# Where the bias of a mixture-of-experts block is put into its accumulators: ahead of all matmuls of a quarter, or token tile by token tile between them

## The chip, the cores and the metric

The kernel runs on the 8 cores of one Trainium2 chip. Each core works on two of the sixteen sequences, alone, with no exchange between cores. The metric is the device time in microseconds (us) of the slowest core.

## The reference, cut to what matters

```python
def ffn(x, Wg, We, be):                 # x: tokens x 1024; We: 8 experts x 1024 x 1024
    gate_logits = xt @ Wg.T
    vals, sel = top_k(gate_logits, 2)
    w = softmax(vals, axis=1)
    y = einsum('td,eod->teo', xt, We) + be[None]
    y_sel = take_along_axis(y, sel[:, :, None], axis=1)
    return einsum('tk,tko->to', w, y_sel)

xn = layernorm(x)
s = attention(xn, qw, kw, vw, ow)       # 16 heads, rotary, causal, 2048 tokens
g = silu(ffn(xn, Wg, We, be))
out = x + s * g
```

The kernel computes all eight experts for each token and weighs them with a matrix `wm` that is zero for the six that were not chosen. So the output of the block is `sum over e of wm[t,e] * (xn @ We[e].T)` plus the bias part `wm @ be`, and it is the bias part that this case is about.

## The kernel before

A core has 4096 tokens, 32 tiles of 128. The program is one list of instructions, written out in order; `W(engine, instruction, waits, inc)` appends to it (line 57, `emit`), and each engine then runs its own in that order. A wait is on a count of a semaphore: `eT` counts TensorE's instructions, `eA` ScalarE's, `eV` VectorE's, and each transfer family has one of its own. A wait for a count that the same engine has already waited for is dropped.

Three stages follow one another with barriers between them:

1. Layer norm, transposition of the tokens into `xnT`, the projections to q, k and v, the rotary embedding, and then the gate's logits and weights `wm` (lines 243 to 614).
2. The experts (lines 625 to 706), which are the stage of the change.
3. Attention, the output projection and the product with the gate (from line 713).

In stage 2 a loop over `q4` takes four quarters of 8 token tiles. The accumulators `acc32[t8]` (128 tokens x 1024 f32, eight of them) live in SBUF. A quarter has three parts:

- **Bias phase**, lines 629 to 642: for each of the 8 tiles and 2 halves (512 columns) TensorE multiplies an 8-row weight matrix `wmT` with the 8x512 bias `be16s` into the one PSUM tile `PC6` (L632), and ScalarE copies `PC6` into the accumulator (L637). Since there is one `PC6`, each of the 16 matmuls waits for the copy before it (`("eA", C["eA"])`), and each copy for its matmul. `bias_done` is the count of the 16th copy.
- **Expert passes**, lines 643 to 696: `eg` takes two experts at a time. SyncE's queue brings their weights with 16 transposing transfers (L654, in the profile as SPq L237) into a pair of slots; there are two pairs, so pass `eg` uses the pair that pass `eg-2` left. The first matmul of a pass waits for all 16 (`(swx, wrd)`). Each of the 8 tiles and 2 halves then takes 16 matmuls of 128x128 by 512 columns (L677), in turn into `PA` and `PB`, and VectorE adds the two results with their gate weights to the accumulator (L687). In the first pass (`eg == 0`) the first matmul of a half also waits for `bias_done`, and so does VectorE.
- **Gate phase**, lines 697 to 706: ScalarE takes the SiLU of each accumulator (L701) into one of two staging tiles, and SyncE's queue stores it to `g_sp` (in the profile as SPq L238). A SiLU waits until the store of two tiles ago has landed.

ScalarE's order is: 8 SiLUs of a quarter, then the 16 copies of the next one. SyncE's order is: 8 stores of a quarter, then the transfers of the first pass of the next one, which have their slots free since pass 2 of the quarter before.

Of the kernel before, what the change touches and what calls it, by code (L numbers as in the profile page):

```python
# [107 lines left out]
def build_nc():  # L108
# [24 lines left out]
    with ctx:  # L133
# [33 lines left out]
        acc32 = [c32(AR2, 65536 + 4096 * i, 1024) for i in range(8)]  # L167
# [17 lines left out]
        wmT = sbt("wmT", [8, NT * 128], F16)  # L185
# [4 lines left out]
        be16s = sbt("be16s", [8, D], F16)  # L190
# [27 lines left out]
        PC6 = ctx.enter_context(nc.psum_tensor("PC6", [128, 512], F32))[:]  # L218
# [12 lines left out]
        W = P.emit  # L231
        C = P.cnt

        def dma(q, out, in_, sem, transpose=False, waits=()):
# [6 lines left out]
        tok = {}  # L241
# [14 lines left out]
          waits=[("scst", cst)], inc="eV")  # L256
        W("vector", lambda e: e.tensor_sub(wgr[0:8, :], wgf[0:8, :],
                                           wgs[0:8, 0:D]),
          waits=[("eV", C["eV"])], inc="eV")
        W("vector", lambda e: e.tensor_copy(wgs[0:8, D:2 * D], wgr[0:8, :]),  # L260
          waits=[("eV", C["eV"])], inc="eV")
        W("vector", lambda e: e.tensor_sub(wgr[0:8, :], wgr[0:8, :],
                                           wgs[0:8, D:2 * D]),
          waits=[("eV", C["eV"])], inc="eV")
        W("vector", lambda e: e.tensor_copy(wgs[0:8, 2 * D:3 * D], wgr[0:8, :]),
          waits=[("eV", C["eV"])], inc="eV")
        wg_split = C["eV"]
        for c in range(NCH):
            for s3 in range(3):
# [5 lines left out]
                  waits=[("eV", wg_split), ("scst", cst), ("eA", C["eA"])],  # L275
                  inc="eT")
# [4 lines left out]
                  waits=[("eT", C["eT"])], inc="eA")  # L281
# [261 lines left out]
        for t in range(NT):  # L543
            for c in range(NCH):
                for s3 in range(3):
# [5 lines left out]
                          start=(c == 0 and s3 == 0),  # L551
                          stop=(c == NCH - 1 and s3 == 2)),
                      waits=[("eA", max(C["eA"] if t == 0 and c == 0 and s3 == 0 else 0, wgT_done))], inc="eT")
        W("vector", lambda e: e.tensor_copy(lgall[:, :], PC6[:, 0:256]),
          waits=[("eT", C["eT"]), ("eV", C["eV"])], inc="eV")
# [3 lines left out]
          waits=[("eT", C["eT"]), ("eV", C["eV"])], inc="eV")  # L559
        W("vector", lambda e: e.reduce_max(v1a[:, :], d3(lgall), axis=AX.X),  # L560
          waits=[("eV", C["eV"])], inc="eV")
        W("vector", lambda e: e.tensor_tensor(
            d3(eq16[:, 0:256]), d3(lgall), bc(v1a[:, :]), op=ALU.is_equal),
          waits=[("eV", C["eV"])], inc="eV")
# [60 lines left out]
        bew = C["sbe"]  # L625
        wew = C["swe"]
        slot_free = {}
        for q4 in range(4):
            for t8 in range(8):
                gt = q4 * 8 + t8  # L630
                for half in range(2):
                    W("tensor", lambda e, gt=gt, half=half: e.matmul(  # L632
                        PC6[:, :], wmT[0:8, gt * 128:(gt + 1) * 128],
                        be16s[0:8, half * 512:(half + 1) * 512],
                        start=True, stop=True),
                      waits=[("sbe", bew), ("eA", C["eA"])], inc="eT")
                    W("scalar", lambda e, t8=t8, half=half: e.copy(  # L637
                        acc32[t8][:, half * 512:(half + 1) * 512],
                        PC6[:, :]),
                      waits=[("eT", C["eT"]),  # L640
                             ("eA", tok.get(("accfree", t8), 0))], inc="eA")
            bias_done = C["eA"]
            for eg in range(4):
                e0, e1 = 2 * eg, 2 * eg + 1
                sp = eg % 2
                slots = (weT[2 * sp], weT[2 * sp + 1])
                swx = "sweA" if sp == 0 else "sweB"
                ldw = [("eT", max(slot_free.get(sp, 0), loopT)),
                       ("eV", loopV), ("eP", loopP), ("swe", wew),
                       ("scsA", C["scsA"]), ("scsB", C["scsB"]),  # L650
                       ("scsC", C["scsC"]), ("scsD", C["scsD"])]
                for (sl, ee) in ((slots[0], e0), (slots[1], e1)):
                    for c in range(NCH):
                        dma("sync", sl[:, c * D:(c + 1) * D],  # L654
                            we16[ee, :, c * 128:(c + 1) * 128], swx,
                            transpose=True, waits=ldw)
                        ldw = []
                wrd = C[swx]
                for t8 in range(8):
                    gt = q4 * 8 + t8  # L660
                    for half in range(2):
                        bk = (t8 * 2 + half) % 2
                        PG = PA if bk == 0 else PB
                        for c in range(NCH):
                            lhs = xnT[:, c * T + gt * 128:
                                      c * T + (gt + 1) * 128]
                            for ib in range(2):
                                wts = [(swx, wrd)]
                                if c == 0:
                                    wts.append(  # L670
                                        ("eV", tok.get(("pbfree", 2 * bk + ib),
                                                       0)))
                                    if eg == 0 and ib == 0:
                                        wts.append(("eA", bias_done))
                                W("tensor",
                                  lambda e, ib=ib, lhs=lhs, c=c, PG=PG,
                                  sl=slots[ib], half=half: e.matmul(  # L677
                                      PG[:, 512 * ib:512 * ib + 512], lhs,
                                      sl[:, c * D + half * 512:
                                         c * D + (half + 1) * 512],  # L680
                                      start=(c == 0), stop=(c == NCH - 1)),
                                  waits=wts, inc="eT")
                        mm = C["eT"]
                        for ib, ee in ((0, e0), (1, e1)):
                            W("vector",
                              lambda e, ib=ib, t8=t8, half=half, PG=PG,
                              gt=gt, ee=ee: e.scalar_tensor_tensor(  # L687
                                  acc32[t8][:, half * 512:(half + 1) * 512],
                                  PG[:, 512 * ib:512 * ib + 512],
                                  wm32[:, gt * 8 + ee:gt * 8 + ee + 1],  # L690
                                  acc32[t8][:, half * 512:(half + 1) * 512],
                                  op0=ALU.mult, op1=ALU.add),
                              waits=[("eT", mm), ("eA", bias_done),
                                     ("eV", C["eV"])], inc="eV")
                            tok[("pbfree", 2 * bk + ib)] = C["eV"]
                slot_free[sp] = C["eT"]
            for t8 in range(8):
                gt = q4 * 8 + t8
                p = gt % 2
                sg_ = "sgsA" if p == 0 else "sgsB"  # L700
                W("scalar", lambda e, t8=t8, p=p: e.activation(  # L701
                    g_st[p][:, :], acc32[t8][:, :], AF.Silu),
                  waits=[("eV", C["eV"]), (sg_, 16 * (gt // 2))], inc="eA")
                tok[("accfree", t8)] = C["eA"]
                dma("sync", g_sp[gt * 128:(gt + 1) * 128, :], g_st[p][:, :],
                    sg_, waits=[("eA", C["eA"])])
# [294 lines left out]
```

How the kernel before makes its waits and increments, by code:

```python
            def body(eng):  # L84
                for (e, ws, fn, incs) in ops:
                    if e != name:
                        continue
                    for (sn, v) in ws:
                        eng.wait_ge(sems[sn], v)
                    if fn is None:
                        if incs:
                            ins = eng.drain()
                            for (sn, a) in incs:
                                ins.then_inc(sems[sn], a)
                        continue
                    ins = fn(eng)
                    for (sn, a) in incs:
                        ins.then_inc(sems[sn], a)
```

## Time and profile before

| | |
|---|---|
| time, median of 3 runs | 2890.38 us (2868.5, 2890.38, 3182.27) |
| profiled execution, its own time | 2858.58 us |
| its span, slowest core (core 3) | 2857.0 us |
| spans of the eight cores | 2838.1 to 2857.0 us |
| TensorE matmul busy | 2176.7 us (76%) |
| VectorE, ScalarE, GpSimd busy | 35%, 34%, 16% |
| stage 2 (experts), from the first bias matmul to the end of the last matmul | 587 to 1634 us |

The span runs from the first to the last instruction of the slowest core. In the rows PE is TensorE's matmuls, PEld its weight loads, DVE is VectorE, ACT ScalarE, POOL GpSimd, and SPq the queue in which SyncE issues transfers. The granted clock of TensorE is given as a share of full speed: 1.00 is 2.4 GHz, 0.50 is 1.2 GHz. "Idle before <- X" is the time for which the engine stood still before this instruction, and what ended it.

### The profile page before, as it was taken

To read this page: it belongs to the slowest core of one execution; us is meant where nothing else is said; L and a number is where in the kernel's file an instruction comes from. 1 tells how busy PE (TensorE), PEld (TensorE's weight loads), DVE (VectorE), ACT (ScalarE), POOL (GpSimd) and SP (SyncE) were. 2 spreads that over 40 slices of the span, in tenths; PEclk is the share of its full clock that TensorE was granted. 3 is DMA by queue.
4 is the path that set the end of the run, shared out by engine and by line. 5 is a ranking of instruction groups with operands and counts; after the bars stand their busy time and mean duration, and the time that the engine had idled before them with its cause. 6 is when DMAs were issued, how large, how long until landed. Compare 5 with 4: busy or idle time off the path is not lost.

```text
span 2857.0 us, 30318 instructions; the slowest of 8 cores (2838.1 to 2857.0 us)
## 1 busy us (share of the span) xinstructions
PE 2176.7 (76%) x9976; PEld 818.2 (29%) x9976; DVE 996.4 (35%) x1529; ACT 961.7 (34%) x1373; POOL 461.2 (16%) x543
## 2 busy tenths in 40 slices
PE   1888788569977995999599806777788347677787
PEld 0333333424433442444144301121211102121211
DVE  3675776424422442344144303231201213221212
ACT  2444443110010002000200015657587134657574
POOL 0465665300000000000000002211111021211110
PEclk9999999679988997999699955888898757788888
DMA  4299842714416524560743080211010532020100
GB/s 130 75 164 169 156 107 85 125 29 60 60 44 104 78 41 89 80 97 1 132 75 59 14 218 6 74 42 32 14 46 1 136 72 74 1 74 1 59 1 30
DMA packets 382533, 203.94 MB, mean 71 GB/s; under 512 B 342944, under 2 KB 351136, under 8 KB 381872
## 3 DMA queue, kind: packets, MB, share of 16 engines
q1 hardware_dynamic: 370160, 142.76, 25.5%
q0 software_dynamic: 12224, 59.27, 9.7%
q8 instruction: 85, 1.39, 0.2%
q14 instruction: 64, 0.52, 0.1%
HBM read 84.28 MB, written 67.37 MB: 53 GB/s over the span
## 4 chain that ended last, share of the span: by engine, by line
PE 60%; ACT 12%; issue 7%; SPq 7%; POOL 5%; DVE 4%; DMA 3%; ACTq 0%; POOLq 0%; DVEq 0%
PE PA L677 16%; PE PB L677 15%; ACT AR L861 9%; SPq L237 6%; PE PV L780 6%; POOL AR L872 5%; PE PA L906 5%; PE PA L419 4%; PE PB L419 4%; PE PC L419 4%; PE PA L851 2%; PE PB L851 2%; ACT AR L790 2%; PE PV L359 1%; DMA AR<-c_sin 1%
## 5 line engine op out<-in xcount | busy, mean ns | idle before, releaser
L677 PE MATMUL PA<-AR 128*128 128x512 f16 x2048 | 472.1, 384 | 22.4 <-DMA AR<-we 21.5
L780 PE MATMUL PV<-AR 128*128 128x512 f16 (+6 forms) x1280 | 417.0, 417 | 66.7 <-POOL AR L872 66.6
L677 PE MATMUL PB<-AR 128*128 128x512 f16 x2048 | 462.9, 379 | 0.0
L861 ACT ACTIVATE AR<-PA 128x1024 f16<-128x1024 f32 x320 | 303.1, 947 | 249.3 <-PE PA L851 247.1
L851 PE MATMUL PA<-AR 64*128 64x512 f16 x640 | 148.6, 455 | 292.1 <-ACT AR L861 142.4
L687 DVE SCALAR_TENSOR_TENSOR AR<-PA,wm,AR 128x512 f32<-128x512 f32 x256 | 192.2, 751 | 416.4 <-PE PA L677 226.2
L861 ACT ACTIVATE AR<-PB 128x1024 f16<-128x1024 f32 (+1 forms) x320 | 276.2, 863 | 90.3 <-PE PB L851 89.6
L872 POOL TENSOR_TENSOR AR<-AR,tri 128x256 f16<-128x256 f16 x256 | 170.7, 667 | 814.9 <-ACT AR L861 791.0
L677 PEld LDWEIGHTS PA<-AR 128*128 128x128 f16 x2048 | 202.5, 99 | 271.8 <-issue 36.4
L687 DVE SCALAR_TENSOR_TENSOR AR<-PB,wm,AR 128x512 f32<-128x512 f32 x256 | 192.2, 751 | 250.3 <-PE PB L677 232.2
L822 DVE TENSOR_TENSOR AR<-AR,PC 64x512 f16<-64x512 f32 x64 | 43.5, 680 | 662.4 <-PE PC L816 661.3
L701 ACT ACTIVATE AR<-AR 128x1024 f16<-128x1024 f32 x32 | 32.1, 1049 | 711.3 <-DVE AR L687 696.1
L677 PEld LDWEIGHTS PB<-AR 128*128 128x128 f16 x2048 | 200.4, 98 | 241.6
L419 PE MATMUL PC<-AR 128*128 128x512 f16 x512 | 194.8, 380 | 0.0
L238 POOL DMA_DIRECT2D AR<-v_sp x2 | 2.4, 1196 | 1143.9 <-ACTq L92 1118.9
L851 PEld LDWEIGHTS PA<-AR 64*128 64x128 f16 x640 | 36.3, 96 | 465.0 <-issue 464.2
L419 PE MATMUL PA<-AR 128*128 128x512 f16 x512 | 160.3, 394 | 0.0
L802 DVE COPY AR<-PV 64x1024 f32<-64x1024 f32 x64 | 77.9, 1217 | 233.0 <-PE PV L780 227.2
L780 PEld LDWEIGHTS PV<-AR 128*128 128x128 f16 (+1 forms) x1280 | 83.3, 104 | 264.3 <-issue 264.0
L419 PE MATMUL PB<-AR 128*128 128x512 f16 x512 | 156.2, 385 | 0.0
L906 PE MATMUL PA<-AR 128*128 128x512 f16 x512 | 133.9, 421 | 17.5 <-DVE AR L828 14.8
L851 PE MATMUL PB<-AR 64*128 64x512 f16 x640 | 146.9, 453 | 0.0
(99 smaller groups left out, 1693.2 us busy)
## 6 DMA issues: line engine op xcount, KB each, us to landing
we<-we POOLq DMA_DIRECT2D x8, 2048.0 KB, 23.8
out_c<-AR SPq DMA_DIRECT2D x8, 2048.0 KB, 9.1
v_sp<-AR POOLq DMA_DIRECT2D x32, 264.0 KB, 3.5
AR<-v_sp POOLq DMA_DIRECT2D x2, 4224.0 KB, 26.3
AR<-x_c SPq DMA_DIRECT2D x32, 256.0 KB, 11.6
k_sp<-AR POOLq DMA_DIRECT2D x32, 256.0 KB, 4.4
q_sp<-AR SPq DMA_DIRECT2D x32, 256.0 KB, 3.7
g_sp<-AR SPq DMA_DIRECT2D x32, 256.0 KB, 2.0
```

The lines of the kernel that those rows point to most:

```text
L237: return e.dma_start(out, in_, transpose=True)
L419: e.matmul(o_, lhs, rhs, start=(c == 0), stop=(c == NCH - 1)),
L677: sl=slots[ib], half=half: e.matmul(PG[:, 512 * ib:512 * ib + 512], lhs, sl[:, c * D + half * 512: c * D + (half + 1) * 512], start=(c == ...
L687: gt=gt, ee=ee: e.scalar_tensor_tensor(acc32[t8][:, half * 512:(half + 1) * 512], PG[:, 512 * ib:512 * ib + 512], wm32[:, gt * 8 + ee:gt * ...
L780: nkc=nkc, p2=p2, mw=mw: e.matmul(PV2[0:mw, 512 * p2 + w0:512 * p2 + 512], v_sb[:, kc * VF + h * VW:kc * VF + h * VW + mw], expb3[sbk][:, ...
L790: W("scalar", lambda e: e.activation(recL[64:65, 0:1024], PV2[64:65, 0:1024], AF.Ln), waits=[("eT", pvmm), ("eA", C["eA"]), ("eA", tok.get ...
L802: W("vector", lambda e: e.tensor_copy(at2[0:64, :], PV2[0:64, 0:1024]), waits=[("eT", pvmm), ("eV", tok.get("atrd", 0))], inc="eV")
L822: W("vector", lambda e, hp=hp: e.tensor_mul(attnT[0:64, hp * 512:(hp + 1) * 512], at2[0:64, 0:512], PC6[0:64, :]), waits=[("eV", tok[("atv ...
L851: pbuf=pbuf, PS=PS, p2=p2: e.matmul(PS[:, 512 * p2:512 * p2 + 512], kT[base:base + 64, ch * S + kc * 128:ch * S + (kc + 1) * 128], qT[pbuf ...
L861: W("scalar", lambda e, PS=PS, sbk=sbk, ev=ev: e.activation(ev(expb3[sbk]), ev(PS), AF.Exp, scale=1.0 / 32.0), waits=[("eT", C["eT"]), ("e ...
L872: W("gpsimd", lambda e, sbk=sbk, tv=tv: e.tensor_mul(tv(expb3[sbk]), tv(expb3[sbk]), tri[:, :].unsqueeze(1).broadcast_to([128, 2, 128])), ...
L906: e.matmul(PA[:, 512 * half:512 * half + 512], attnT[0:128, cp * 512 + jt * 128: cp * 512 + (jt + 1) * 128], ow128[:, cp * D + half * 512: ...
```

## The change

The bias matmul and its copy move into a small function `bias_init(t8, half)`, which is called twice for each tile inside the first expert pass, just ahead of that tile's matmuls. The bias phase at the head of a quarter is gone. The single wait for `bias_done` becomes a wait for the copy of the tile and half in question. Numbers and kinds of instructions stay: 64 bias matmuls and 64 copies over the program; `PC6` stays the one PSUM tile for both halves, so the second bias matmul of a tile waits for the copy of the first.

```diff
         for q4 in range(4):
-            for t8 in range(8):
+            def bias_init(t8, half, q4=q4):
                 gt = q4 * 8 + t8
-                for half in range(2):
-                    W("tensor", lambda e, gt=gt, half=half: e.matmul(
-                        PC6[:, :], wmT[0:8, gt * 128:(gt + 1) * 128],
-                        be16s[0:8, half * 512:(half + 1) * 512],
-                        start=True, stop=True),
-                      waits=[("sbe", bew), ("eA", C["eA"])], inc="eT")
-                    W("scalar", lambda e, t8=t8, half=half: e.copy(
-                        acc32[t8][:, half * 512:(half + 1) * 512],
-                        PC6[:, :]),
-                      waits=[("eT", C["eT"]),
-                             ("eA", tok.get(("accfree", t8), 0))], inc="eA")
-            bias_done = C["eA"]
+                W("tensor", lambda e, gt=gt, half=half: e.matmul(
+                    PC6[:, :], wmT[0:8, gt * 128:(gt + 1) * 128],
+                    be16s[0:8, half * 512:(half + 1) * 512],
+                    start=True, stop=True),
+                  waits=[("sbe", bew), ("eA", C["eA"])], inc="eT")
+                W("scalar", lambda e, t8=t8, half=half: e.copy(
+                    acc32[t8][:, half * 512:(half + 1) * 512],
+                    PC6[:, :]),
+                  waits=[("eT", C["eT"]),
+                         ("eA", tok.get(("accfree", t8), 0))], inc="eA")
+                tok[("accinit", t8, half)] = C["eA"]
...
                 for t8 in range(8):
                     gt = q4 * 8 + t8
+                    if eg == 0:
+                        bias_init(t8, 0)
+                        bias_init(t8, 1)
                     for half in range(2):
...
                                     if eg == 0 and ib == 0:
-                                        wts.append(("eA", bias_done))
+                                        wts.append(
+                                            ("eA", tok[("accinit",
+                                                        t8, half)]))
...
-                              waits=[("eT", mm), ("eA", bias_done),
+                              waits=[("eT", mm),
+                                     ("eA", tok[("accinit", t8, half)]),
                                      ("eV", C["eV"])], inc="eV")
```

## Rows read from the trace of the kernel before

**Rows 1.** The page, parts 1, 2 and 4: busy time, slices, chain by engine.
```profile
PE 2176.7 (76%) x9976; PEld 818.2 (29%) x9976; DVE 996.4 (35%) x1529; ACT 961.7 (34%) x1373; POOL 461.2 (16%) x543
...
PE   1888788569977995999599806777788347677787
...
PE 60%; ACT 12%; issue 7%; SPq 7%; POOL 5%; DVE 4%; DMA 3%; ACTq 0%; POOLq 0%; DVEq 0%
```

**Rows 2.** Groups by line in stage 2: busy and mean; idle before, releasers.
```profile
L677 PE MATMUL PA<-AR 128*128 128x512 f16 x2048 | 472.1, 384 | 22.4 <-DMA AR<-we 21.5 <-ACT AR L637 0.8
L637 ACT COPY AR<-PC 128x512 f32<-128x512 f32 x64 | 37.5, 586 | 54.7 <-PE PC L632 54.7
L632 PE MATMUL PC<-be16s,wmT 8*128 8x512 f16 x64 | 37.1, 580 | 95.3 <-ACT AR L637 50.9 <-ACT AR L701 43.0 <-POOLq L92 1.4
```

**Rows 3.** Timeline of the first bias phase and first matmuls: start, us, engine, line.
```profile
587.05 0.58 PE L632 MATMUL PC<-be16s,wmT 8*128 8x512 f16 x1 [1.41 <-POOLq L92]
587.72 0.59 ACT L637 COPY AR<-PC 128x512 f32<-128x512 f32 x1 [1.73 <-PE PC L632]
...
588.45 0.58 PE L632 MATMUL PC<-be16s,wmT 8*128 8x512 f16 x1 [0.82 <-ACT AR L637]
...
609.45 5.53 PE L677 MATMUL PA<-AR 128*128 128x512 f16 x16 [0.82 <-ACT AR L637]
...
618.27 3.62 PE L677 MATMUL PA<-AR 128*128 128x512 f16 x16
618.61 1.60 DVE L687 SCALAR_TENSOR_TENSOR AR<-PB,wm,AR 128x512 f32<-128x512 f32 x2 [1.78 <-PE PB L677]
```

**Rows 4.** Timeline between the first and the second quarter, all engines.
```profile
836.82 11.15 SPq L238 DMA_DIRECT2D g_sp<-AR  x8
...
845.58 2.01 ACT L701 ACTIVATE AR<-AR 128x1024 f16<-128x1024 f32 x2 [1.29 <-DMA g_sp<-AR]
847.70 0.10 PEld L632 LDWEIGHTS PC<-be16s,wmT 8*128 8x128 f16 x1 [15.66 <-issue]
847.73 0.58 PE L632 MATMUL PC<-be16s,wmT 8*128 8x512 f16 x1 [15.19 <-ACT AR L701]
...
869.88 0.59 ACT L637 COPY AR<-PC 128x512 f32<-128x512 f32 x1 [0.82 <-PE PC L632]
...
878.12 6.02 PE L677 MATMUL PA<-AR 128*128 128x512 f16 x16 [8.33 <-DMA AR<-we]
```

**Rows 5.** Chain that ended last, 864 to 880 us: start, us, what.
```profile
871.07 1.87 SPq L237
...
872.99 4.78 DMA AR<-we
877.77 0.35 issue
878.12 2.29 PE PA L677 x5
```

**Rows 6.** Who waited for whom, second and third of these boundaries: us, times, longest.
```profile
PE PC L632 <- ACT AR L637: 13.0, 15, 1.2
...
PE PA L677 <- DMA AR<-we: 5.9, 1, 5.9
...
PE PC L632 <- ACT AR L637: 12.8, 15, 0.9
...
PE PA L677 <- DMA AR<-we: 7.3, 1, 7.3
```

**Rows 7.** Line 677 by line: durations min/median/max and first and last start.
```profile
L677 PE MATMUL PA<-AR x2048: 379/379/634, 609.4 to 1630.5; 128*128 128x512 f16 x187
```

**Rows 8.** Chain that ended last, whole span: one half's matmuls at full clock.
```profile
618.43 3.45 PE PA L677 x16
```

**Rows 9.** Windows: span, PE, PEld, DVE, ACT, POOL busy, granted clock, DMA share, GB/s.
```profile
300.00:400.00 100.00, 87.30 (x412) 38.64 (x411) 75.11 (x122) 45.84 (x101) 63.08 (x62) 1.00 0.80 151
...
586.00:609.00 23.00, 9.25 (x16) 1.60 (x16) 0.00 (x0) 9.07 (x16) 0.00 (x0) 0.50 0.00 0
...
870.00:878.00 8.00, 0.00 (x0) 0.00 (x0) 0.00 (x0) 0.46 (x1) 0.00 (x0) 0.50 1.22 161
878.10:883.00 4.90, 4.88 (x12) 1.87 (x13) 0.00 (x0) 0.00 (x0) 0.00 (x0) 0.50 1.10 180
883.00:933.00 50.00, 50.00 (x233) 22.63 (x232) 21.36 (x29) 0.00 (x0) 0.00 (x0) 1.00 0.33 61
...
1999.40:2002.50 3.10, 2.98 (x8) 0.50 (x8) 0.00 (x0) 2.58 (x3) 0.00 (x0) 0.50 0.00 0
```

**Rows 10.** Timeline of TensorE in stage 1, between two tiles of projections.
```profile
307.32 0.27 PE L359 MATMUL PV<-idn,AR 128*128 128x128 f16 x2
308.01 0.35 PE L359 MATMUL PV<-idn,AR 128*128 128x128 f16 x2 [0.42 <-DVE AR L370]
309.45 0.39 PE L359 MATMUL PV<-idn,AR 128*128 128x128 f16 x2 [1.09 <-ACT AR L369]
310.15 0.39 PE L359 MATMUL PV<-idn,AR 128*128 128x128 f16 x2 [0.31 <-DVE AR L370]
```

**Rows 11.** Timeline of TensorE in stage 3, around the tail of a head pair.
```profile
1996.13 0.37 PE L816 MATMUL PC<-AR,ones 1*64 1x512 f16 x1
1996.43 0.39 PE L851 MATMUL PA<-AR 64*128 64x512 f16 x2
1996.66 0.38 PE L851 MATMUL PB<-AR 64*128 64x512 f16 x2
1999.52 0.61 PE L851 MATMUL PA<-AR 64*128 64x512 f16 x2 [2.48 <-ACT AR L861]
```

**Rows 12.** Timeline of SyncE's queue, several stretches: start, us, transposing transfers.
```profile
848.07 24.87 SPq L237 DMA_TRANSPOSE AR<-we  x15
...
666.87 24.36 SPq L237 DMA_TRANSPOSE AR<-we  x15
...
936.01 22.62 SPq L237 DMA_TRANSPOSE AR<-we  x16
...
529.15 52.75 SPq L237 DMA_TRANSPOSE AR<-we  x32
```

## The prediction

> **What bounds the kernel now.** I read the page first: its busy times, its slices and the shares of the chain [rows 1]. TensorE is busy for 76% of the span and carries 60% of the chain, and the slices show it at 9 through the middle of the run, which is the expert stage, with single dips. No other engine passes 35%. So in the expert stage I ask only where TensorE stands still.
>
> The groups by line answer that [rows 2]. Over the stage the big matmuls L677 wait 22.4 us in all, and 21.5 of them for the expert weights. The bias matmuls L632 wait 50.9 us for the copy before them and 43.0 us for the SiLUs. The reader is to see that the copies' 50.9 us look like the prize, and that a second releaser, the weights, ends the wait of L677 after them.
>
> So the timelines come next, at two kinds of place. **First quarter** [rows 3]: the first bias matmul starts at 587.05, the next at 588.45, a cycle of 1.40 us, and the sixteenth copy lets the first big matmul go at 609.45. That is 16 x 1.40 = 22.4 us in which TensorE waits for nothing but this chain: SyncE's queue had issued the first 32 weight transfers from 529.15 to 581.90 [rows 12], and in the bias phase the DMA share is 0.00 [rows 9]. **The three later quarters**, of which the second stands for all [rows 4]: the last SiLU lets the first bias matmul go at 847.73, the last copy ends at 870.47, and still the first big matmul starts only at 878.12, 8.33 us after TensorE could have, released by the weights. The chain of waits shows the same from the other end [rows 5]: back from 878.12 it goes to the landing of a weight transfer, to SyncE's queue, and never touches the bias phase. In the other two boundaries the weights come 5.9 and 7.3 us after the bias [rows 6]. The sum of the three, 21.5 us, is the 21.5 of [rows 2]. The queue can't start earlier: the transfers stand behind the eight stores of the gate, the last of which is issued when the last SiLU is done [rows 4].
>
> **The change part by part.**
>
> *Removed: the bias phase in front of each quarter.* In quarter one it takes 22.4 us off the path. In quarters two to four it takes nothing off: the bias ran in the shade of the weights, from 847.73 to 870.47, and without it the first big matmul still waits for 878.12. That cover is what makes the old place cheap there.
>
> *Added: a pair of bias matmuls and copies in front of each tile of the first pass.* TensorE is in order, so behind the second bias matmul of a tile stand the 32 big matmuls of that tile, and behind them VectorE. The steps for one tile, at full clock:
> - the first bias matmul follows the matmuls before it directly; its wait was met a tile ago. A 512-column matmul takes 0.38 us from start to end then [rows 7]; the bias matmul itself shows 0.58, but only at half clock [rows 3, 9].
> - 0.09 us to the copy (588.45 minus 0.14 minus 0.59 is 587.72, and the matmul ends at 587.63), the copy 0.59, and 0.14 to the second bias matmul [rows 3].
> - So start to start 0.38 + 0.09 + 0.59 + 0.14 = 1.20 us.
> - the second bias matmul holds the stream for one slot: 3.45 / 16 = 0.216 us [rows 8]. Its copy runs under the first half's 16 big matmuls (3.45 us against about 0.7) and the second half finds it done.
>
> Together 1.41 us a tile. The first tile of a quarter is apart: in quarters two to four its pair runs before the weights land and costs nothing. In quarter one it runs at half clock: 1.40 + 0.43 = 1.83 us.
>
> *Moved waits.* VectorE and the big matmuls get one wait more per half, already met. VectorE stands still for 1.78 us of each 3.45 [rows 3], so it never comes late. ScalarE has nothing else to do in a pass. No transfer is issued in another order; the weights of the third pass start when the first pass ends, some 10 us later on the clock but at the same distance from their use.
>
> *The sum.*
> - Quarter one: -22.4 + 1.83 + 7 x 1.41 = -10.7 us.
> - Quarters two to four: 3 x 7 x 1.41 = +29.6 us.
> - Together +18.9 us, or 28 x c + 1.8 - 22.4 with c = 1.41.
>
> *Bounds of the unshown cost c.* No row shows a bias matmul inside a running stream. From below it is 1.41: each term is the shortest of its kind in the trace. A gain is excluded, since the wait of the second matmul for the copy is in the code. From above I take the half-clock pair, 1.83, and two changes between a small and a full weight tile at 0.09 each (the matmul at 1996.43 stands 0.30 behind a one-row matmul at 1996.13 where a slot is 0.216 [rows 11]): 2.0 us. That gives 28 x 2.0 + 1.8 - 22.4 = +35.4 us. I take 1.41, since the row it is nearest to is the full-clock stream.
>
> *The clock.* TensorE's clock falls to half after long idle: it is at 0.50 through 870 to 878 and for the first 4.9 us of matmuls after it [rows 9]. The new stalls are 0.82 us long (1.20 less the matmul's 0.38), one in about 8.3 us. In stage 1 TensorE has idle stretches of 0.42, 1.09 and 0.31 us between two tiles [rows 10], and the clock is 1.00 over 300 to 400 [rows 9], with 87% busy. In stage 3 a wait of 2.48 us [rows 11] is followed by 3.1 us at 0.50 [rows 9]. The new stall is shorter than the 1.09 us that stage 1 shows at 1.00. I cost it at nothing and keep the fall as a rival.
>
> The Trainium skill, "TensorE: Matmul & The Clock Gate", section "A second HAM failure mode: psum-queue depth-cycling", speaks against this change: it says that a TensorE which often idles briefly between groups of matmuls, because of how PSUM is cycled, can swing between half and full clock and lose throughput. By that rule the sum would be that of the rival "the clock falls" below; stage 1, with its brief idle stretches at 1.00, doesn't bear it out.
>
> **Which total.** The profiled execution took 2858.6 us, its span and 1.6 us around it. The three runs gave 2868.5, 2890.4 and 3182.3; I leave the last out as disturbed. The mean of the other two and the profiled one is 2872.5, which is 14 above the profiled time and 18 below the median. I add to that: 2872.5 + 18.9 = **2891.4 us**. Against the profiled time alone it would be 2877.5, against the median 2909.3; the spread of the base is wider than the effect.
>
> **The rivals.**
> - *All four bias phases come off the path.* This is what the 50.9 us of [rows 2] suggest: -4 x 22.4 + 4 x 1.83 + 28 x 1.41 = -42.8, so 2829.7 us, 1.5% faster. It decides where weights land before the bias is done. Against it: the weights were last at three of three boundaries, by 8.3, 5.9 and 7.3 us. This is the case on the other side. Chance 3%.
> - *The weights land sooner once bias and copies are out of their way.* Beside the bias phase 15 transfers were issued in 24.87 us, 1.66 each; at 936.01 sixteen took 22.62, 1.41 each [rows 12]. At best 15 x 0.25 = 3.7 us a boundary, 11 in all: +8 instead of +19, 2880 us. Against it: at 666.87, beside full matmuls and no bias, 15 took 24.36. To turn the sign it would need 6.3 us a boundary. Chance 12%.
> - *The clock falls in the stalls.* A return from half clock costs 9 to 12 matmuls at 0.21 us more each (5.53 us for sixteen at 609.45 [rows 3] against 3.45 is 2.1; 6.02 at 878.12 [rows 4] is 2.6). At 28 stalls that is 59 to 73 us on top of 18.9, 78 to 92: about 2957 us, 3.0% slower. Against it: stage 1. For it: the 2.48 us case. It decides where the granted clock of the first passes shows below 1.00. Chance 7%.
>
> **How the numbers follow.** My forecast, +18.9 to +35.4, has 78%. The predicted time is 2891 us. For the range: low is the smallest base with the weights-sooner case, 2858.6 + 8 = 2866; high is the largest undisturbed base with the upper bound of c, 2890.4 + 35.4 = 2926. Outside are the 3%, the 7%, and some 8% for executions that drift further (the clock in stage 3 wanders, and a shift of its start may move it). 2% of 2890 is 58 us, about what a measurement of this kernel can tell from no change. Neither my forecast nor the first two rivals reach it; only the clock does. So faster 2%, within 2% 90%, slower 8%.
>
> **What would show it.** In the profile of the changed kernel:
> - the first big matmul of quarter one starts near 589, not 609;
> - at the three later boundaries it is still released by the weights, and the wait named there grows from 21.5 us to about 21.5 + 3 x 21 = 85 us, since TensorE now stops 14 matmuls earlier;
> - inside each first pass TensorE waits some 0.8 us for L637, once a tile, and the first pass takes about 10 us more than the second;
> - the granted clock stays at 1.00 in it.
> It would be wrong if the stall of a tile is much over 1.4 us, if the clock in the first pass is below 1.00, or if the first big matmul of the later quarters comes closer to the last SiLU than 30 us.

## The result, and the profile after

The changed kernel is slower by 1%: its time is 1.0097 times that of the kernel before, 95% interval 1.0069 to 1.0126. On a base of 2872 us, the one used in the prediction, that is +28 us (20 to 36). The medians of 42 executions each are 2909.32 us after and 2888.37 us before; some executions of either kernel are held up by a lower clock on one die, and the ratio leaves these out.

| | before | after |
|---|---|---|
| profiled execution, its own time | 2858.58 us | 2880.76 us |
| its span, slowest core | 2857.0 us (core 3) | 2879.2 us (core 0) |
| stage 1, to the first bias matmul, mean of eight cores | 583.3 us | 579.0 us |
| stage 2, from there to the start of the last half's big matmuls | 1040.2 us | 1066.6 us |
| stage 3, the rest | 1225.0 us | 1226.7 us |
| big matmuls waiting for weights, mean of eight cores | 16.3 us | 76.3 us |

The three stages are read from the first and last starts of the bias and of the big matmuls on each core, so stage 3 here begins with the last quarter's gate phase. The whole loss is in stage 2: +26.4 us.

First the groups by line in stage 2 of the changed kernel (busy, mean ns, idle before and its releasers). L681 is the big matmul, L631 the bias matmul, L636 its copy; they answer to [rows 2].

```profile
L681 PE MATMUL PA<-AR 128*128 128x512 f16 x2048 | 473.0, 385 | 77.6 <-DMA AR<-we 77.6
...
L636 ACT COPY AR<-PC 128x512 f32<-128x512 f32 x64 | 37.5, 585 | 302.5 <-PE PC L631 302.5
```

Line 631 by itself, on the same core: durations and what its engine waited for.

```profile
L631 PE MATMUL PC<-be16s,wmT x64: 371/384/581, 588.6 to 1484.8; 8*128 8x512 f16 x64
...
  ACT AR L706: 42.5, 3
  ACT AR L636: 27.9, 32
```

Two things moved against [rows 2]. The wait for the copies fell from 50.9 us to 27.9, as the change meant. The wait for the weights rose from 21.5 (core 3) to 77.6 (core 0): TensorE only reaches it earlier.

The timeline shows where the time went. First quarter, core 0, all engines (start, us, engine, line), to be laid beside [rows 3]:

```profile
588.64 0.58 PE L631 MATMUL PC<-be16s,wmT 8*128 8x512 f16 x1 [1.44 <-POOLq L92]
...
590.56 5.68 PE L681 MATMUL PA<-AR 128*128 128x512 f16 x16
...
599.62 0.38 PE L631 MATMUL PC<-be16s,wmT 8*128 8x512 f16 x1
...
600.10 0.58 ACT L636 COPY AR<-PC 128x512 f32<-128x512 f32 x1 [8.80 <-PE PC L631]
600.80 0.09 PEld L631 LDWEIGHTS PC<-be16s,wmT 8*128 8x128 f16 x1 [1.09 <-issue]
600.83 0.37 PE L631 MATMUL PC<-be16s,wmT 8*128 8x512 f16 x1 [0.82 <-ACT AR L636]
601.13 3.14 PEld L681 LDWEIGHTS PA<-AR 128*128 128x128 f16 x16 [0.24 <-issue]
601.13 3.63 PE L681 MATMUL PA<-AR 128*128 128x512 f16 x16
...
604.38 3.33 PEld L681 LDWEIGHTS PB<-AR 128*128 128x128 f16 x16
604.60 3.62 PE L681 MATMUL PB<-AR 128*128 128x512 f16 x16
...
609.65 3.14 PEld L681 LDWEIGHTS PA<-AR 128*128 128x128 f16 x16 [0.24 <-issue]
609.66 3.63 PE L681 MATMUL PA<-AR 128*128 128x512 f16 x16
```

The first big matmul comes 1.92 us after the first bias matmul, where it was 22.4. From then on a tile takes 8.52 us (601.13 to 609.65) and two halves of big matmuls fill 6.91 of them, so the pair costs c = 1.61 us.

Second quarter, TensorE on core 3, to be laid beside [rows 4]:

```profile
830.36 0.58 PE L631 MATMUL PC<-be16s,wmT 8*128 8x512 f16 x1 [15.05 <-ACT AR L706]
831.82 0.58 PE L631 MATMUL PC<-be16s,wmT 8*128 8x512 f16 x1 [0.88 <-ACT AR L636]
856.66 6.02 PE L681 MATMUL PA<-AR 128*128 128x512 f16 x16 [24.26 <-DMA AR<-we]
862.52 3.62 PE L681 MATMUL PB<-AR 128*128 128x512 f16 x16
866.07 0.39 PE L631 MATMUL PC<-be16s,wmT 8*128 8x512 f16 x1
867.33 0.37 PE L631 MATMUL PC<-be16s,wmT 8*128 8x512 f16 x1 [0.88 <-ACT AR L636]
867.63 3.63 PE L681 MATMUL PA<-AR 128*128 128x512 f16 x16
```

The bias phase is gone and the weights are last all the same, 26.3 us after the first bias matmul. The other seven pairs now stand behind them, each with a stop of 0.88 us. That it was 0.82 in the first quarter is a matter of the quarter and not of the core; core 0 in the second quarter:

```profile
880.01 0.37 PE L631 MATMUL PC<-be16s,wmT 8*128 8x512 f16 x1 [0.88 <-ACT AR L636]
880.32 3.63 PE L681 MATMUL PA<-AR 128*128 128x512 f16 x16
```

All eight cores have c = 1.61 us in the first quarter and 1.67 in the later ones. Why the step from copy to matmul is 0.06 us longer there was not looked into. The clock in this pass and in the next one, as windows (span, busy times, granted clock after the last "x0)"):

```profile
866.00:925.00 59.00, 52.86 (x235) 22.29 (x235) 21.02 (x28) 8.21 (x14) 0.00 (x0) 1.00 0.23 41
925.00:978.00 53.00, 53.00 (x247) 24.01 (x246) 22.51 (x30) 0.00 (x0) 0.00 (x0) 1.00 0.48 80
```

It stays at 1.00 through the stops.

### The profile page after: what moved, and what is told of

Its sections match the earlier page's. It is cut to its first block, busy times and chain, and to the rows that moved or that the text cites. A ratio compares the mean times of both kernels' runs of the same rounds, so it can differ in the third digit from the quotient of the medians.

```text
span 2879.2 us, 30378 instructions; the slowest of 8 cores (2867.2 to 2879.2 us)
## 1 busy us (share of the span) xinstructions
PE 2166.5 (75%) x9976; PEld 814.9 (28%) x9976; DVE 990.7 (34%) x1529; ACT 962.3 (33%) x1373; POOL 462.1 (16%) x543
## 4 chain that ended last, share of the span: by engine, by line
PE 60%; ACT 13%; issue 7%; SPq 7%; POOL 5%; DVE 4%; DMA 3%; ACTq 0%; POOLq 0%; DVEq 0%
PE PA L681 16%; PE PB L681 15%; ACT AR L866 8%; PE PV L785 6%; SPq L237 6%; POOL AR L877 5%; PE PA L911 5%; PE PA L419 4%; PE PB L419 4%; PE PC L419 4%; PE PA L856 2%; PE PB L856 2%; ACT AR L795 2%; PE PV L359 1%; DMA AR<-c_sin 1%
## 5 line engine op out<-in xcount | busy, mean ns | idle before, releaser
L681 PE MATMUL PA<-AR 128*128 128x512 f16 x2048 | 473.0, 385 | 77.6 <-DMA AR<-we 77.6
L681 PE MATMUL PB<-AR 128*128 128x512 f16 x2048 | 462.9, 379 | 0.0
L681 PEld LDWEIGHTS PA<-AR 128*128 128x128 f16 x2048 | 200.3, 99 | 327.6 <-issue 99.1
L681 PEld LDWEIGHTS PB<-AR 128*128 128x128 f16 x2048 | 200.4, 98 | 241.6
L911 PE MATMUL PA<-AR 128*128 128x512 f16 x512 | 133.6, 420 | 16.3 <-DVE AR L833 14.4
## 6 DMA issues: line engine op xcount, KB each, us to landing
we<-we POOLq DMA_DIRECT2D x8, 2048.0 KB, 25.7
```

Of the source, the lines that this page charges most:

```text
L681: sl=slots[ib], half=half: e.matmul(PG[:, 512 * ib:512 * ib + 512], lhs, sl[:, c * D + half * 512: c * D + (half + 1) * 512], start=(c == ...
L911: e.matmul(PA[:, 512 * half:512 * half + 512], attnT[0:128, cp * 512 + jt * 128: cp * 512 + (jt + 1) * 128], ow128[:, cp * D + half * 512: ...
```

## The experiments

The kernels are variants of the changed one unless it is said otherwise. Lengths of stages are means over the eight cores of the profiled execution, as in the table above. A summary first:

| | ratio to before, 95% interval | stage 2 | against before's 1040.2 |
|---|---|---|---|
| changed kernel | 1.0097 [1.0069, 1.0126] | 1066.6 us | +26.4 |
| e1, change in quarter one only | 0.9963 [0.9924, 1.0003] | 1032.2 us | -8.0 |
| e2, change in quarters two to four only | 1.0104 [1.0033, 1.0175] | 1073.3 us | +33.1 |
| e3, one bias matmul per half, no stop for the copy | 1.0009 [0.9970, 1.0048] | 1046.3 us | +6.1 |
| e5, kernel before with early weights | 0.9945 [0.9888, 1.0003] | 1026.8 us | -13.4 |
| e6, changed kernel with early weights | 0.9866 [0.9768, 0.9965] | 989.7 us | -50.5 |
| e7, e3 with early weights and early SiLU | 0.9618 [0.9549, 0.9688] | 929.4 us | -110.8 |
| e9, e7 without the wait for the SiLU | 0.9465 [0.9341, 0.9588] | 913.4 us | -126.8 |

### e1 and e2: the change cut in two

The condition is `q4 > 0` in e1, as shown, and `q4 == 0` in e2: where it holds, the bias phase stays in front.

```diff
+            if q4 > 0:
+                for t8 in range(8):
+                    bias_init(t8, 0)
+                    bias_init(t8, 1)
...
-                    if eg == 0:
+                    if eg == 0 and not (q4 > 0):
```

> The change in the first quarter alone; quarters two to four keep the bias phase in front. Theory (the weights hide the phase in the later quarters, each tile of the stream costs c): the first quarter's 22.4 us give way to 1.9 us for the cold first pair and 7 x 1.61 us read from the changed kernel, so 9 us faster than before, ratio 0.997. The wait of the big matmuls for the weights stays what it was, about 15 to 21 us in three. Rival (the +28 us come from elsewhere than the later quarters, as from attention or from ScalarE): no faster than before, ratio 1.00 to 1.01.

> The change in quarters two to four alone; the first quarter keeps its bias phase in front. Theory: 3 x 7 tiles x 1.65 us = 35 us slower than before, less up to 2 us if the weights land a little sooner, ratio 1.012; together with e1 it makes the whole change (35 - 9 = 26). Rival (weights land much sooner without the bias beside them): under 25 us slower, and the first big matmul comes under 25 us after the first bias matmul.

Measured: e1's stage 2 is 8.0 us shorter than before, e2's 33.1 us longer. They add to +25.1, the changed kernel's own +26.4 within what cores differ by. So the change is a gain of some 8 us in the one quarter whose bias phase nothing hid, and a loss of 33 us, 11 a quarter, in the three where the weights hid it. The groups by line show the weights' wait, in e1 as in [rows 2], in e2 as in the changed kernel; the first row is e1's, the second e2's:

```profile
L688 PE MATMUL PA<-AR 128*128 128x512 f16 x2048 | 471.9, 384 | 21.3 <-DMA AR<-we 21.3
```

```profile
L688 PE MATMUL PA<-AR 128*128 128x512 f16 x2048 | 472.4, 384 | 79.1 <-DMA AR<-we 78.3 <-ACT AR L636 0.8
```

The ratio of e1 alone can't be told from 1; it is its stage 2 that carries the verdict. e2's can. In e2 the loss is under the 35 us expected but over the rival's 25. What is missing is the weights: they let the first big matmul go 26.7 us after the first bias matmul, in the mean of cores and boundaries, against 27.6 before, which makes 2.6 us over three boundaries.

### e3: what in a pair costs time

```diff
-                    if eg == 0:
-                        bias_init(t8, 0)
-                        bias_init(t8, 1)
                     for half in range(2):
+                        if eg == 0:
+                            bias_init(t8, half)
...
-                                    if eg == 0 and ib == 0:
-                                        wts.append(
-                                            ("eA", tok[("accinit",
-                                                        t8, half)]))
```

> As the changed kernel, but one bias matmul stands before each half (not two before a tile) and the big matmuls no longer wait for the copy, which only VectorE needs. Nothing is left out. Theory (the stall for the copy of the one PSUM tile is 0.82 us of the 1.61, and two changes of weight tile size at about 0.18 a bias matmul the rest): a tile costs 2 x 0.40 = 0.79 us, no wait for ScalarE in the passes; first quarter -16 us, later ones +18 us, so within 3 us of before and 25 us faster than the changed kernel, ratio to before 1.000 to 1.001. Rival (the cost is the matmuls' place and not their wait): it stays 24 us or more slower than before.

Measured: ratio 1.0009, stage 2 +6.1 us against before, 20.3 us shorter than in the changed kernel. TensorE in the first quarter:

```profile
603.02 3.63 PE L676 MATMUL PA<-AR 128*128 128x512 f16 x16
606.58 0.39 PE L631 MATMUL PC<-be16s,wmT 8*128 8x512 f16 x1
606.90 3.63 PE L676 MATMUL PB<-AR 128*128 128x512 f16 x16
610.46 0.39 PE L631 MATMUL PC<-be16s,wmT 8*128 8x512 f16 x1
610.78 3.63 PE L676 MATMUL PA<-AR 128*128 128x512 f16 x16
```

No row has a wait. A half takes 3.88 us (603.02 to 606.90) instead of 3.45, so a bias matmul costs 0.43 us and a tile 0.85, where 0.79 was expected. So spreading the pair and dropping the stop saves 1.61 to 1.67 less 0.85, 0.76 to 0.82 us a tile. What remains, 0.43 us for a matmul whose slot is 0.216, is twice the slot, and that is the question of the next experiment. Stage 2 was expected within 3 us of before and is 6 above: 32 x 0.06 = 1.9 us of that is the dearer bias matmul, and 1.8 the weights, which were last 0.6 us later a boundary than before (28.2 against 27.6).

### e4 and e8: 8 rows against 128

```diff
-                    PC6[:, :], wmT[0:8, gt * 128:(gt + 1) * 128],
-                    be16s[0:8, half * 512:(half + 1) * 512],
+                    PC6[:, :], xnT[:, gt * 128:(gt + 1) * 128],
+                    xnT[:, half * 512:(half + 1) * 512],
```

> As the changed kernel, but the matmul of the bias uses 128 rows of the tokens instead of the 8 rows of the gate weights and the bias, so the accumulators start from a wrong value; same place, same waits, same 512 columns. Theory (about 0.09 us is lost at each change between an 8-row and a 128-row weight tile, since the weight load isn't pulled ahead): spacing of the second of the pair to the next big matmul falls from 0.30 to 0.22 us, a tile from 1.61 to about 1.44 us. Rival (the 0.18 us belong to the wait or to the change of PSUM tile): spacing stays 0.30.

The records of e4 are from an execution at a granted clock of 0.81 in the expert passes, so its spacings can't be laid beside the changed kernel's. The same kernel was taken once more:

> The same kernel as e4 (accumulators start from a wrong value), taken once more, since e4's records are at a granted clock of 0.81. At 1.00 in the first pass, theory (change between weight tiles of 8 and of 128 rows costs): the second of the pair is followed by the next big matmul after 0.22 us or less (0.30 in the changed kernel), the first follows the stream at once, a tile costs about 1.44 us. Rival: 0.30 and 1.61 to 1.67 us as in the changed kernel.

e8, core 3, TensorE in the second quarter, at 1.00, to be laid beside the changed kernel's rows of the same core above:

```profile
868.13 0.38 PE L631 MATMUL PC<-AR 128*128 128x512 f16 x1 [0.88 <-ACT AR L636]
868.35 3.61 PE L681 MATMUL PA<-AR 128*128 128x512 f16 x16
871.80 3.62 PE L681 MATMUL PB<-AR 128*128 128x512 f16 x16
875.25 0.38 PE L631 MATMUL PC<-AR 128*128 128x512 f16 x1
876.51 0.38 PE L631 MATMUL PC<-AR 128*128 128x512 f16 x1 [0.88 <-ACT AR L636]
876.73 3.61 PE L681 MATMUL PA<-AR 128*128 128x512 f16 x16
```

The second of the pair is followed after 0.22 us (0.30 in the changed kernel), the first starts one slot behind the stream (871.80 + 3.45 = 875.25; in the changed kernel 862.52 + 3.45 = 865.97 and the start at 866.07), and a tile takes 8.38 us, c = 1.47, against 8.56 to 8.58 and 1.67 in this quarter. The stop of 0.88 us is the same. So 0.20 us of c are the two changes between a weight tile of 8 rows and one of 128. In the changed kernel's rows of the first quarter it can be seen how: the weight load of the big matmul behind the pair starts at 601.13, together with its matmul, where in the running stream it goes ahead (604.38 for the matmul at 604.60). In e8 it goes ahead behind the pair too, 0.12 us before the matmul at 868.35:

```profile
868.23 3.24 PEld L681 LDWEIGHTS PA<-AR 128*128 128x128 f16 x16
```

With that every part of c is measured: two slots (0.43), two changes of weight tile (0.20), and the stop. The stop costs more than the 0.76 to 0.82 that e3 saved, because e3's two separate bias matmuls pay four changes of weight tile where the pair pays two. The second matmul of the pair starts 1.20 us (first quarter) or 1.26 us (later) after the first, instead of 0.216, so the stop takes 0.98 or 1.05 us. Stage 2 of e8 is 1061.3 us, 5.3 less than the changed kernel's, where 28 x 0.20 = 5.6.

### e5 and e6: is the place bad, or the weights?

In both, the transfers for a quarter's first pass are issued before the stores of the gate, at the head of pass four, as soon as pass three has left their slots.

```diff
+                if not (q4 > 0 and eg == 0):
+                    load_w(eg)
                 wrd = C[swx]
+                if eg == 3 and q4 < 3:
+                    load_w(0)
```

> As the kernel before, with one thing moved: the weight transfers of a quarter's first pass are issued ahead of the eight stores of the gate, at the end of pass three, so that they land under pass four. Theory (weights were last at the three later boundaries by 5 to 8 us and the bias is next behind them): the wait of the big matmuls for weights goes to 0, they are released by the last copy, and the gain is only 15 to 21 us, ratio 0.993. Rival (the transfers cost the same elsewhere, by slowing the stores or pass four): no gain.

> As the changed kernel, with the same move of the weight transfers. Theory (the weights are all that made the old place of the bias free): now the removed bias phase is time on the path, each later boundary loses about 26 us and keeps 7 x 1.65 us in the pass; against before 3 x (-28 + 2) + 35 - 9 = -52 us, ratio 0.982; against e5, the same change is worth about -36 us where it cost 28. Rival (the change is bad in itself): e6 slower than e5.

e5, groups by line: the wait for weights is gone and the last copy releases the big matmuls, four times:

```profile
L698 PE MATMUL PA<-AR 128*128 128x512 f16 x2048 | 470.9, 384 | 3.3 <-ACT AR L652 3.3
```

Stage 2 is 13.4 us shorter. That is before's 16.3 us of waiting for weights less 3 x 0.8 for the copies that are last now: the bias phase had ended some 5 us ahead of the weights, so no more was to be had from them.

e6, TensorE between the first and the second quarter:

```profile
809.22 3.62 PE L691 MATMUL PB<-AR 128*128 128x512 f16 x16
828.07 0.58 PE L647 MATMUL PC<-be16s,wmT 8*128 8x512 f16 x1 [15.24 <-ACT AR L716]
829.53 0.58 PE L647 MATMUL PC<-be16s,wmT 8*128 8x512 f16 x1 [0.88 <-ACT AR L652]
830.04 5.82 PE L691 MATMUL PA<-AR 128*128 128x512 f16 x16
```

The first big matmul now comes 1.97 us after the first bias matmul, close to the 1.92 of quarter one. Stage 2 is 50.5 us shorter than before (52 expected). The same change, laid on the kernel with early weights, gives 1026.8 - 989.7 = 37 us; laid on the kernel as it was, it took 26. This is the case's main finding, and it is shown: neither the pairs nor their stops differ between the two (from first to last big matmul the four quarters grow by 46.5 us over e5's here, and by 47.2 over before's in the changed kernel), only what stood behind the bias phase. The ratio of e6 (0.9866, 38 us) is less than its stage 2 says: stage 3 took 1233.5 us in the profiled executions of e5 and e6, 8.5 more than before, with the same instructions (more on that at the end).

### e7 and e9: all of it together

The SiLU and the store of a tile stand right behind its last addition in pass four; the loop over them at the end of a quarter is gone.

```diff
+                    if eg == 3:
+                        p = gt % 2
+                        sg_ = "sgsA" if p == 0 else "sgsB"
+                        W("scalar", lambda e, t8=t8, p=p: e.activation(
+                            g_st[p][:, :], acc32[t8][:, :], AF.Silu),
+                          waits=[("eV", C["eV"]), (sg_, 16 * (gt // 2))],
+                          inc="eA")
+                        tok[("accfree", t8)] = C["eA"]
+                        dma("sync", g_sp[gt * 128:(gt + 1) * 128, :],
+                            g_st[p][:, :], sg_, waits=[("eA", C["eA"])])
```

> The spread bias of e3, the early weights of e5, and the SiLU and store of a tile right behind its last addition in pass four. Nothing is left out. Theory: TensorE no longer stops between quarters (42 to 46 us each, and about 2.4 us of half clock after each), nor for the last eight SiLUs (11 us), nor for the first bias phase (22 us), and pays 32 x 0.79 = 25 us: about 145 us faster than before, ratio 0.95. Rival (something else is next, stores and weights of eight cores at once or VectorE): under 100 us.

Measured: ratio 0.9618, about 109 us (89 to 129), stage 2 -110.8 us, and the mean span of the cores 122 us under before's. In the 122 is what the last eight SiLUs gave, which lie outside stage 2: the last one ends 3.3 us after the last big matmul, where it was 13.7. That is short of the 145 expected, and over the rival's 100 by stage 2 and the spans, though the interval of the ratio reaches below it. The boundary shows the main cause:

```profile
819.47 3.62 PE L686 MATMUL PB<-AR 128*128 128x512 f16 x16
826.21 0.37 PE L647 MATMUL PC<-be16s,wmT 8*128 8x512 f16 x1 [3.13 <-ACT AR L709]
826.52 5.31 PE L686 MATMUL PA<-AR 128*128 128x512 f16 x16
```

TensorE still stops for 3.13 us (3.1 to 3.4 at the three boundaries), for the SiLU of the last tile, and its clock falls: sixteen matmuls take 5.31 us and not 3.45. Three times both is about 15 us of the 23 that are missing. A smaller part is that the three boundaries of the kernel before, from the last big matmul of a quarter to the first of the next, come to 125 us, and the expectation counted 42 to 46 each. The stop shown above, as windows:

```profile
816.00:823.00 7.00, 7.00 (x33) 3.04 (x31) 3.00 (x4) 1.06 (x1) 0.00 (x0) 1.00 0.11 39
826.20:829.00 2.80, 2.79 (x7) 0.96 (x8) 0.00 (x0) 0.59 (x1) 0.00 (x0) 0.57 0.64 155
829.00:831.80 2.80, 2.80 (x12) 1.08 (x10) 0.00 (x0) 0.00 (x0) 0.00 (x0) 0.82 1.07 102
```

That stop is no need of TensorE's: the bias matmul waits for all that ScalarE had been given, and needs only its PSUM tile. In e9 `tok["pc6"]` is the count of the last copy out of `PC6`.

```diff
-                  waits=[("sbe", bew), ("eA", C["eA"])], inc="eT")
+                  waits=[("sbe", bew), ("eA", tok["pc6"])], inc="eT")
```

> As e7, but a bias matmul waits only for the last copy out of its own PSUM tile and not for all that ScalarE was given before it, the SiLU above all. Nothing is left out. Theory (after e7 the 3.1 us that TensorE stands still for the SiLU at each boundary are the last stop between quarters, and only VectorE needs that order): the wait for the SiLU goes, TensorE stops under 1.5 us a boundary, 6 to 9 us faster than e7, ratio to before 0.958 to 0.960. Rival (PSUM: the first sums of a quarter wait for VectorE instead): same time as e7, with the wait moved to the big matmuls.

```profile
803.84 3.62 PE L688 MATMUL PB<-AR 128*128 128x512 f16 x16
807.39 0.39 PE L648 MATMUL PC<-be16s,wmT 8*128 8x512 f16 x1
807.71 3.63 PE L688 MATMUL PA<-AR 128*128 128x512 f16 x16
811.27 0.39 PE L648 MATMUL PC<-be16s,wmT 8*128 8x512 f16 x1
```

The boundary has vanished: 0.10 us beyond the slot. Stage 2 is 16.0 us shorter than e7's, twice what was expected, since the expectation had the stops (3 x 3.1) and left out the clock (3 x 1.9). Both together are 15. With a ratio of 0.9465, 5% under the kernel before, e9 is the best version here; by the mean spans of the profiled executions, 2718.7 against 2848.6 us, it is 4.6%.

## Why the prediction was right, point by point

The forecast of +18.9 us, with +35.4 as its upper bound, met +28 by the ratio and +26.4 in stage 2; the mechanism was right and one term was too small.

- *The bias phase was on the path in quarter one alone.* Right, by e1 and by the timelines. The first pair cost 1.92 us where 1.83 was said.
- *The weights stay last at the three later boundaries.* Right: their wait rose by 60.0 us in the mean of the cores (16.3 to 76.3), where 63 was said. The total said, 85 us, was too high only because it started from core 3, the core that had waited longest (21.5 us against a mean of 16.3). One reading was a little off: the big matmul could not have started 8.33 us earlier, since its copy ended 0.8 us into that wait. The cover was 7.5 us there and (16.3 - 3 x 0.8) / 3 = 4.6 us in the mean, which is what e5 got back.
- *c = 1.41 us a tile.* Too small; it measured 1.61 in the first quarter and 1.67 in the later ones. This is the term that was mis-sized. The prediction held the two changes of weight tile of 0.09 us in its upper bound and not in its value; e8 shows them to be real, 0.20 us together. The rest, in the later quarters, is the step from copy to matmul, 0.88 us there and 0.82 in the first. With these the sum becomes 7 x 1.61 + 21 x 1.67 + 1.9 - 22.4 = +25.8, and stage 2 measured +26.4.
- *The clock holds.* Right: 1.00 through a pass with a stop of 0.88 us in each 8.6. The rival had 7%. What the Trainium skill warns of ("TensorE: Matmul & The Clock Gate", "A second HAM failure mode: psum-queue depth-cycling"), a TensorE that idles briefly and often between groups of matmuls and loses its clock by it, did not come true for stops of this length and spacing. The single stop of 3.13 us in e7, after which the clock fell, is another case than the frequent brief ones of that section.
- *The weights land sooner.* Not in the changed kernel. From first bias matmul to first big matmul of the later quarters it was 27.6 us before and 27.5 after, in the mean of cores and boundaries, where the rival's bound was 3.7 us less. Single boundaries lie between 25.7 and 30.6 us in these two executions, and e2 has a mean of 26.7, so a shift of 1 us can't be told from how executions differ.
- *All four phases come off the path.* Not so here; e6 is the kernel in which they do, and it has the gain that this rival named: 37 us, against 42.8 by the small c.
- *What would show it.* The signs named came true: the first big matmul at 590.56, the weights last at the three boundaries, one stop a tile in the first pass, the clock at 1.00. From first to last big matmul the first quarter grew by 11.5 us and the others by 11.9 each, where 10 was said for the first pass. A tile's 1.61 to 1.67 us is over the 1.4 that was named as a limit, but not by much. A further sign of being wrong, a first big matmul closer to the last SiLU than 30 us, came true as well (27.5 us) and means nothing: before the change the mean was 27.6. The 30 was read from the first boundary of core 3 (30.4 us), and the other two of that same core have 28.2 and 29.4.
- *The total.* 2891 us was said, and the 42 executions have a median of 2909, the lowest 2877. The base of 2872.5 was 16 us under the median of the 42 executions before, 2888. The medians differ by 21 us, close to the 18.9 said, and that closeness is luck: the ratio and stage 2 give 26 to 28.

The account of stage 2 closes. The big matmuls of the four quarters take 47.2 us longer, from first to last of each quarter; the first of them comes 20.5 us sooner in quarter one (22.40 to 1.91 us after the first bias matmul) and 0.3 us sooner in the three others together. That is the +26.4.

## What to carry to other kernels

A phase that nothing hides at one boundary can be free at the next; ask at each what would have released the engine had the phase been absent, and price the removal there at the difference, not at the phase's length. Moving hidden work into the stream of the engine that bounds the kernel costs its full length each time, and here more than that: a stop for a one-buffer round trip (TensorE idle for 0.8 to 0.9 us, its stream 1.0 us longer) and the change of weight tile (0.2 us). Look for what stands behind the phase first: the same edit that cost 26 us gave 37 once the weights were issued ahead of the stores.

## What the runs showed of the hardware that was not expected

- A 512-column matmul with 8 rows in the midst of 128-row ones costs 0.43 us of TensorE at full clock, twice its slot of 0.216 (e3); with 128 rows the pair's surplus of 0.20 us is gone (e8).
- A single stop of 3.13 us in a dense stream (clock 1.00 and TensorE busy throughout 816 to 823) brought the clock down, and the sixteen matmuls behind it took 1.86 us more (e7); a stop of 0.88 us in each 8.6 did not. Between the two, stage 3 of the kernel before has one of 2.48 us, followed by a clock of 0.50 [rows 9, 11]; TensorE had been idle for part of the time ahead of it as well, so the two can't be compared by their lengths alone.
- Stage 3 took from 1215.6 us (e7) to 1233.5 us (e5, e6) in the mean of eight cores, 1225.0 before and 1228.1 in e9. In e7 and e9 it holds 10.4 us less, since most of the last quarter's SiLUs are done by then. The attention and all behind it, the same instructions in all kernels, take 1150 us in the mean before, in the changed kernel and in e7, 1155 in e5 and e6, and 1160 in e9. That goes with the granted clock of single cores. Two cores of e9 as windows over this part, core 2 and then core 4:

```profile
1558.00:2709.00 1151.00, 819.68 (x3200) 207.81 (x3200) 253.41 (x320) 674.17 (x769) 182.94 (x271) 0.79 0.17 42
1558.00:2725.00 1167.00, 850.50 (x3198) 209.37 (x3196) 253.52 (x320) 680.71 (x769) 183.13 (x271) 0.73 0.17 41
```

Cores at 0.78 to 0.79 take 1146 to 1156 us for it, those at 0.73 to 0.74 take 1160 to 1169. Why a core is granted less, no run here shows. The spread is half of the effect first predicted, in a stage that the changes do not touch, and the reason that the comparisons here go by stage 2.
